# Edge tables of a four-layer graph network: the weighting of a piece's upper half moved from VectorE to GpSimd, and a new order of GpSimd's work

## What is computed

```
def spmm(edge_row, edge_col, edge_val, m):
    gathered = edge_val[:, None] * m[edge_col]
    return jax.ops.segment_sum(gathered, edge_row, num_segments=N_NODES)
...
x = _layernorm(x + _L0_gnn_ref(x, src, dst, edge_weight, ...))   # two weighted sums over the edges
x = _layernorm(x + _L1_gnn_ref(x, ..., src, dst, edge_type_8))   # sum by relation
x = _layernorm(x + _L2_gnn_ref(x, W, b, src, dst, edge_weight))  # hyperbolic, weighted sum
x = _layernorm(x + _L3_gnn_ref(x, edge_index, ...))              # attention over the edges
```

## Time and profile before

| | us |
|---|---|
| median of 3 runs | 9356.58 |
| lowest and highest run | 9354.81, 9357.62 |
| span of the profiled execution | 12999.9 |
| start of the first one-hots (L720) in it | 125.9 |
| last save of a table (L912) starts | 807.11 |

### The profile page before, as it was taken

The page is one execution under the profiler, slowest core; times in us unless marked ns, Lnnn a source line. Parts: engine busy times, 40 slices in busy tenths (PEclk is TensorE's granted clock), DMA queues, the critical chain, the costliest instruction groups (busy, mean ns, idle before and its releaser), DMA issues. The chain is left out here.

```text
span 12999.9 us, 294862 instructions
## 1 busy us (share of the span) xinstructions
PE 9231.9 (71%) x88712; PEld 7531.3 (58%) x88762; DVE 6869.4 (53%) x25269; ACT 3183.5 (24%) x9441; POOL 5674.7 (44%) x5790
## 2 busy tenths in 40 slices
PE   5977777777777777677777774888873555555555
PEld 5866667776766667634454453666662444444443
DVE  8964444444444444456666665555544555555555
ACT  5841111112111111241111123111113233222223
POOL 3534444442444444305555551444442555555552
PEclk8888888888888888789999996888886555555555
DMA  1013333333333333462222223333332111111113
GB/s 50 28 47 90 91 89 89 88 90 105 90 89 90 89 88 90 95 217 69 67 67 66 67 70 110 101 104 102 101 94 70 39 39 39 39 39 39 39 39 61
DMA packets 962709, 999.47 MB, mean 77 GB/s; under 512 B 141701, under 2 KB 861933, under 8 KB 962093
## 3 DMA queue, kind: packets, MB, share of 16 engines
q1 hardware_dynamic: 774502, 616.47, 17.1%
q0 software_dynamic: 174720, 364.70, 12.9%
q10 hardware_dynamic: 13255, 16.19, 0.4%
HBM read 858.52 MB, written 144.69 MB: 77 GB/s over the span
## 5 line engine op out<-in xcount | busy, mean ns | idle before, releaser
L497 POOL DMA_INDIRECT ring<-att_table,idx x1592 | 1556.3, 978 | 1307.7 <-ACT idx L484 715.5
L1225 PE MATMUL psum<-ring 128*128 128x128 bf16 x21276 | 1547.8, 226 | 784.6 <-issue 766.3
L1225 PEld LDWEIGHTS psum<-ring 128*128 128x128 bf16 x21276 | 1281.3, 101 | 984.9 <-issue 927.9
L1162 DVE TENSOR_SCALAR ring<-sel,iota_col 128x640 bf16<-128x640 bf16 (+1 forms) x1576 | 487.0, 369 | 2368.2 <-remote 1627.6
L1240 PE MATMUL psum<-state 64*128 64x128 f32 x14112 | 1479.8, 356 | 208.9 <-issue 206.7
L1240 PEld LDWEIGHTS psum<-state 64*128 64x128 f32 x14112 | 1318.1, 261 | 345.7 <-issue 330.0
L1148 POOL DMA_INDIRECT ring<-gcn_table,idx x980 | 932.3, 951 | 1300.6 <-ACT idx L1197 996.0
L1679 POOL DMA_INDIRECT state<-rel_table,state x1120 | 1071.1, 956 | 981.8 <-ACT state L1779 657.6
L1148 POOL DMA_INDIRECT ring<-rows,idx x980 | 933.7, 953 | 1289.0 <-ACT idx L1197 993.2
L1169 DVE TENSOR_SCALAR state<-iota_row,state 128x128 f32<-128x128 f32 x5488 | 1457.2, 356 | 0.0
L1394 POOL DMA_INDIRECT state<-hyp_table,state x784 | 755.8, 964 | 855.3 <-ACT state L1471 650.6
(11 more groups left out here) (447 smaller groups left out, 15814.7 us busy)
## 6 DMA issues: line engine op xcount, KB each, us to landing
ring<-xparts SPq DMA_DIRECT2D x1332, 192.0 KB
ring<-srow SPq DMA_DIRECT2D x544, 128.0 KB
sel<-drow SPq DMA_DIRECT2D x394, 160.0 KB
sel<-drow SPq DMA_DIRECT2D x394, 128.0 KB
rel_table<-tout SPq DMA_DIRECT2D x98, 512.0 KB, 2.6
ring<-att_table,idx POOLq DMA_INDIRECT x1592
ring<-rows SPq DMA_DIRECT2D x56, 448.0 KB
xparts<-state SPq DMA_DIRECT2D x28, 672.0 KB, 3.6
```

What stands on the lines that cost most here:

```text
L497: pool.indirect_dma_start(out=ring[:, u, k, 0:width], out_offset=None, in_=table, in_offset=bass.IndirectOffsetOnAxis(ap=idx[:, u, k:k + 1 ...
L1162: ins = nc.vector.tensor_scalar(reach[u % 2][:, t, :], wanted[u], at[:, :], None, ALU.is_equal)
L1225: last = nc.tensor.matmul(rowsP[v][:, j * P:(j + 1) * P], reach[v][:, t, j * P:(j + 1) * P], xwin[u][:, t, i, :], start=(t + i == 0), stop ...
```

## The change

The one DVE instruction that weights chunks 14 to 27 is taken out of DVE's loop, with the credit that DVE gave to `weighed` ahead of it. POOL gets it in a function `weigh`, which waits for the group's one-hots and for the build of two groups earlier, and gives the credit. POOL's turn becomes: weighting of g, packing and remainder of g+1, piece g. The last single piece moves behind the eight turns without pieces. The waits of the other engines stay as they are.

```
--- before.py
+++ after.py
@@ -723,7 +723,6 @@
                         ).then_inc(sem("onehot"), 1)
 
                     dve.sem_inc(sem("prod"), 1)
-                    dve.sem_inc(sem("weighed"), 1)
                     one_hot(0, 0)
                     c = Chain(dve, "dve")
                     with dve.Fori(0, GB // 2) as it:
@@ -760,10 +759,6 @@
                                 slots[v], place[1].unsqueeze(2).to_broadcast([P, GC, P]),
                                 iota_row[:, :].unsqueeze(1).to_broadcast([P, GC, P]), ALU.is_equal
                             ).then_inc(sem("slotted"), 1)
-                            nc.vector.tensor_tensor(
-                                marked[v][:, 1, GW:GC, :], hots[v][:, GW:GC, :],
-                                wT[:, bass.ds(g * GC + GW, GC - GW)].unsqueeze(2).to_broadcast(
-                                    [P, GC - GW, AW]), ALU.mult).then_inc(sem("weighed"), 1)
                         c.end()
 
                 @block.gpsimd
@@ -779,6 +774,14 @@
                         nc.gpsimd.tensor_tensor(before_b[:, 1, :], counts_f, before_b[:, 0, :], ALU.subtract
                                                 ).then_inc(sem("resid"), 1)
 
+                    def weigh(g, v):
+                        pool.wait_ge(sem("onehot"), g + 1)
+                        pool.wait_ge(sem("tbuilt"), g + 1)
+                        nc.gpsimd.tensor_tensor(
+                            marked[v][:, 1, GW:GC, :], hots[v][:, GW:GC, :],
+                            wT[:, bass.ds(g * GC + GW, GC - GW)].unsqueeze(2).to_broadcast([P, GC - GW, AW]),
+                            ALU.mult).then_inc(sem("weighed"), 1)
+
                     c = Chain(pool, "pool")
 
                     def piece(j, v, loaded):
@@ -794,18 +797,21 @@
                                                 ALU.subtract).then_inc(sem("parts"), 1)
 
                     pool.sem_inc(sem("resid"), 1)
+                    pool.sem_inc(sem("weighed"), 1)
                     pack(0, 0)
                     with pool.Fori(0, PIECES // 2) as it:
                         c.loop(it, 6)
                         for v in range(2):
+                            weigh(it * 2 + v, v)
+                            pack(it * 2 + (v + 1), 1 - v)
                             piece(it * 2 + v, v, it * 16 + 16)
-                            pack(it * 2 + (v + 1), 1 - v)
                         c.end()
                     c.off, c.n = PIECES // 2 * 6, 0
-                    piece(PIECES - 1, 0, PIECES // 2 * 16 + 16)
                     with pool.Fori(PIECES // 2, GB // 2) as it:
                         for v in range(2):
+                            weigh(it * 2 + v, v)
                             pack(it * 2 + (v + 1), 1 - v)
+                    piece(PIECES - 1, 0, PIECES // 2 * 16 + 16)
 
                 @block.sync
                 def _(sp):
```

More of the change, by code:

```diff
@@ L762, in _ @@
                             ).then_inc(sem("slotted"), 1)
[L763 to L766, removed]
                         c.end()
```

## The result

The changed kernel takes 9424.96 us (median of five runs) against 9357.62 for the kernel before: a ratio of 1.0066, with a 95% interval of 1.0054 to 1.0078, or some 62 to 67 us more. The direction was forecast. The size was not: 9425 lies above the range's end of 9412.

A forecast was written before the change was run, and what follows sets the result against it. The prediction took the SBUF port chain, passed between DVE and POOL, to set the stage's pace. +31 us for 24 pairs and -3 us for groups without pieces gave +28: 9356.6 + 28 = 9385 us, range 9352 to 9412.

The forecast's parts named there:

- The port chain: Edge stage: two-SBUF-operand DVE instructions and casts exclude POOL's, and the reverse; this chain sets the pace, 12.17 and 11.64 us per group.
- L763 leaves DVE, -1.21 and -1.51 us: DVE's loop: removing the weighting takes 1.21 and 1.51 us, instruction and the wait for it, out of a pair's two groups.
- The weighting at 1.52 us: POOL, between piece and packing: the moved weighting adds 1.52 us to the chain, with ends of 1.24 and 1.80.
- The pair at 24.96 to 25.21 us: Loop of 24 pairs with pieces: a pair takes this instead of 23.81 us, taken as +31 us.
- Groups without pieces, -3 us: Eight groups at 11.74 us: chain now 10.5, but PE allows hardly any gain; ends 0 and -10, taken -3 us.
- The last piece was hidden: End of the stage: the moved piece is done by 802, the last build saved at 807.11; uncovered it would cost 4.5 us.
- Sum for the stage: Whole edge stage: +31 for pairs with pieces and -3 for groups without, +28 us.
- I add the difference unscaled to the median: Whole kernel: the stage's +28 us added directly to the median, 9356.6 + 28 = 9385 us.
- faster: Rival: the weighting hides in POOL's idle time, 21.7 us per pair, 59 us saved, 9298 us; chance 0.10.
- No difference: Rival: weighting costs 1.24 us and PE's clock keeps high more often, +14 and a tail of -10, 9361 us; chance 0.26.
- The rival of a much slower kernel: Packing comes late for PE, whose clock falls to 0.50 in both groups, adding 37 us, 9422 us; chance 0.08.
- The rule on who gets the port: Second group: POOL keeps the port between instructions, as the row showed; if first issuer went first, the sum is 8 us lower.

The follow-up runs named there:

- no_weigh: The changed kernel without the weighting on GpSimd, weights of chunks 14 to 27 set to zero once ahead of the loop: ratio 1.0004 to the kernel before, stage 657.5 us.
- credit: The kernel before with the starting credit of `weighed` given by GpSimd instead of VectorE: ratio 1.0019, relation layer 1552.0 us.
- last_piece: The kernel before with only the last single piece moved behind the eight turns without pieces: ratio 0.9999, relation layer 1539.5 us.
- dve_pad5: The changed kernel with five tiny memsets on VectorE behind the stage's loop, putting its later code exactly where it was: ratio 1.0044 to the kernel before.
- psum_before: The kernel before with the row of numbers that L720 and L759 compare with read from PSUM: ratio 0.9969, stage 640.9 us.
- psum_pad4: The changed kernel with the comparison numbers read from PSUM, plus four tiny memsets on VectorE behind the loop: ratio 0.9909 to the kernel before, stage 592.8 us.
- pool_pad: The kernel before with ten tiny memsets added on GpSimd behind the stage's loops: ratio 1.0002, relation layer 1538.7 us.
- psum_after: The changed kernel with the numbers that the one-hots and slots compare with read from PSUM: ratio 0.993 to the kernel before, stage 593.8 us.
- psum_758: The changed kernel with only the slots L758 comparing with numbers in PSUM, the one-hots not: ratio 0.9993 to the kernel before, stage 652.7 us.

## Why the prediction was right in direction and wrong in size

- **The port chain bounds the stage**: right. Operands in PSUM took 41 us from the stage of before and 122 from that of the changed kernel.
- **L763 leaves DVE, -1.21 and -1.51 us**: right, L720 stands at once behind the slots. Two things that L763 did were not counted. The gap between it and L720 was one in which POOL's remainder could get in (caught behind L720 16 times now, twice before), and its time covered part of the way over the remainder and the ranks. L739's wait for the ranks grew from 11.3 to 60.5 us, and is 51.1 in no_weigh, which has no weighting at all. How it divides between the two was not measured.
- **The weighting at 1.52 us**: 1.33 measured. Over 48 groups the sum was 9 us too high by that.
- **The pair at 24.96 to 25.21 us**: 25.27 measured (12.635 per group in the mean, from the second slots to the 48th), against 23.72 before. With the weighting at its real cost the count would have given some 24.7, so the two errors have opposite signs: +31 forecast and +37 measured for the groups with pieces. The missing 14 us lie within what L739's waits grew by.
- **Groups without pieces, -3 us**: they went from 11.43 to 11.12 us, -2 for seven. That is within what the kernel before shows by itself (11.43, 11.44 and 11.74 in three profiles, 12.30 in credit). The last piece was hidden, as said: last_piece shows no cost.
- **Sum for the stage**: +28 forecast, +34.3 measured.
- **"I add the difference unscaled to the median"** is the step that failed. It took the code behind the stage to be as fast as before. The change took five instructions out of VectorE's program, and the relation layer lost 24 us; the attention layer lost 7 more, whose cause is open. dve_pad5 shows the first: with the place restored the layer takes 1536.4 us and the kernel is at +41 us, about 9399 on the old median, which is inside the range. The stage's own 6 us over the forecast would not have left it.
- **The rivals**: POOL's idle room is no room (faster is refuted); the packing was not late for PE. No difference, the rival with 0.26, had the weighting nearly at its price (1.33 against 1.24), but TensorE's clock fell, 0.90 to 0.85, where it was to keep high. The rival of a much slower kernel had the right time, 9422, by luck: PE waited for the packing only at the start of the stage.
- **The rule on who gets the port**: it goes on as the row showed. L792 starts at 413.68, behind L720 at 413.51, and runs its normal 0.39 us while L720 takes 2.00.

## What to carry to other kernels

Before moving work to GpSimd, count what it excludes as well as its idle time: here GpSimd had 45% of the stage free, and yet 1.05 us of each weighting's 1.33 lengthened the stage, until two operands of VectorE were read from PSUM. Look also at what an instruction that you remove was good for: the gap behind it may have let a short, urgent one pass, and its time may have covered another engine's. And after a change to one stage, compare the untouched ones too: here five instructions fewer on VectorE cost 24 us elsewhere, beside the 34 us of the stage that was changed.

## What the runs showed of the hardware

Not expected: the time of a loop depends on where its instructions stand in VectorE's program. In the relation layer the waits of L1693 for which the profile has no cause come 27 times in every kernel. Their sum is 98 to 101 us with the code in its old place, 107 with one instruction fewer ahead, 110 with three and 112 to 113 with four or five; the layer goes with it, from 1536 to 1544 us in the old place to 1552, 1556, 1560 and 1563. One instruction more (psum_before: 102 us, 1543) is not told from none, as psum_pad4 has the same layer time in the old place. Ten instructions more on GpSimd (pool_pad) changed nothing.

That the waits are for the fetching of instructions, after the branch back to the loop's start, is borne out by the packets of the instruction queue, one in each of the 351 waits and 2.4 us ahead of L1693 whatever the kernel. No record says whose instructions a packet carries, and no test changed the packets, so this stays a reading, if a close one. Nor was it tried how the pattern goes on with more instructions added.

The other thing shown is the port. A comparison of VectorE with two operands in SBUF keeps GpSimd's instructions that come behind it waiting; with one of the two in PSUM it takes the same time (3.89 us; 1.57 us, the shortest L720 of the changed kernel being 1.58) and keeps none waiting: the remainder, held up 46 of 57 times in the changed kernel, is held up in none of psum_after.

The attention layer differed too, by 7 to 11 us in three kernels (the changed kernel, credit, psum_758) with VectorE's code at -5, -1 and -4, but not in psum_after at -4, so there the cause stays open.
